# Scores of a head from one 96-row matmul over stacked high and low parts of q and k

## The reference

```python
def _L0_cond_ref(...):                     # layer L0
    q, k, v = x @ Wqkv.T + bqkv            # 16 heads of 32
    attn = softmax(einsum('bhid,bhjd->bhij', q, k) / sqrt(32))
    ...                                    # modulation by coh(x, cond), field term
    return out @ Wout.T + bout
def _L1_cond_ref(...):                     # layer L1: a key mask, no bias
    scores = where(mask, -inf, einsum(q, k) * scale)
    out = (softmax(scores) @ v) @ Wo.T
    return rmsnorm(out) * gain + shift     # the norm is on the output
def _L2_cond_ref(...):                     # layer L2: the norm is on the input
    x = x + attention(rmsnorm(x)) ; return x + swiglu(rmsnorm(x))
x = x + _L0_cond_ref(x, ...); x = x + _L1_cond_ref(x, ...); x = x + _L2_cond_ref(x, ...); ...
```

## Time and profile before

| | us |
|---|---|
| two timed runs | 3266.89 and 3268.45, median 3267.67 |
| profiled execution, span from first to last instruction | 3266.8 |
| TensorE matmul busy | 3106.6 (95%) |
| VectorE / ScalarE / GpSimd busy | 2031.8 (62%) / 1369.6 (42%) / 614.0 (19%) |
| DMA | 216.27 MB, mean 66 GB/s; 22.7% of 16 engines' span |
| one group, L0 / L1 / L2 | 46.6 / 39.9 / 38.1 |

### The profile page before, as it was taken

How to read it: one execution, slowest core, us unless ns; L and a number is a source line. 1 busy time by engine, 2 the same in 40 slices (tenths; PEclk the granted TensorE clock), 3 DMA queues, 4 the chain that set the end, 5 groups by cost and what they waited for, 6 DMA issues and landing times. The chain is left out here.

```text
span 3266.8 us, 64344 instructions
## 1 busy us (share of the span) xinstructions
PE 3106.6 (95%) x24853; PEld 2688.4 (82%) x24853; DVE 2031.8 (62%) x3739; ACT 1369.6 (42%) x2123; POOL 614.0 (19%) x340
## 2 busy tenths in 40 slices
PE   6999999998899999994999999959999999999998
PEld 5989898997788888884888989848888888888886
DVE  5666666665577777775777777755544445556544
ACT  3444444443555555553555555532222223222221
POOL 2112211220122222211111121112222221111111
PEclk8999999999999999997999999979999999999999
DMA  4221222121322222223222222241122232111111
GB/s 153 47 64 51 56 53 64 51 52 48 102 65 64 64 64 64 65 52 110 65 64 71 71 64 71 59 142 52 52 65 72 69 104 73 44 52 39 51 39 39
DMA packets 198918, 216.27 MB, mean 66 GB/s; under 512 B 17537, under 2 KB 173313, under 8 KB 198305
## 3 DMA queue, kind: packets, MB, share of 16 engines
q1 hardware_dynamic: 198816, 214.87, 22.7%
HBM read 122.53 MB, written 41.94 MB: 50 GB/s over the span
## 5 line engine op out<-in xcount | busy, mean ns | idle before, releaser
L783 ACT ACTIVATE L_pth<-L_bank_t 128x512 f16<-128x512 f32 x384 | 227.7, 593 | 380.5 <-PE L_bank_t L614 380.5
L787 ACT ACTIVATE L_shifted<-L_shifted,keep_lift 128x512 f32<-128x512 f32 x384 | 277.2, 722 | 236.6 <-DVE L_shifted L942 234.1
L1516 DVE TENSOR_TENSOR mlp_act_t<-mlp_bank_u,mlp_sg 128x512 f32<-128x512 f32 x128 | 88.5, 691 | 453.3 <-ACT mlp_sg L1418 449.6
L938 DVE TENSOR_REDUCE L_top<-L_bank_s 128x4 f32<-128x512 f32 x384 | 263.1, 685 | 129.5 <-PE L_bank_s L563 65.1
L1418 ACT ACTIVATE mlp_sg<-mlp_bank_g 128x512 f32<-128x512 f32 x128 | 76.6, 598 | 628.6 <-PE mlp_bank_u L1331 628.5
L1558 POOL TENSOR_TENSOR mlp_al<-mlp_act_t,mlp_ah 128x512 fp32r<-128x512 f32 x128 | 175.0, 1367 | 856.3 <-ACT mlp_ah L1424 856.3
L946 DVE TENSOR_TENSOR L_ptl<-L_bank_t,L_pth 128x512 f16<-128x512 f32 x384 | 262.7, 684 | 63.9 <-ACT L_pth L783 60.6
L1121 POOL TENSOR_TENSOR L_vr<-L_vf,keep_v 128x1024 f32<-128x1024 f32 x48 | 99.2, 2067 | 1045.6 <-ACT keep_v L817 1045.6
L630 PEld LDWEIGHTS L_bank_o<-keep_v,L_pth 128*128 128x128 f16 x4608 | 199.0, 96 | 97.6 <-issue 72.6
L942 DVE TENSOR_TENSOR L_shifted<-L_bank_s,L_top 128x512 f32<-128x512 f32 x384 | 265.5, 691 | 16.7
L561 PE MATMUL L_bank_a<-L_xh,L_wkh 128*128 128x256 f32 x768 | 233.7, 304 | 37.7 <-DVE L_wkl L101 24.6
(11 more groups left out here) (272 smaller groups left out, 8925.8 us busy)
## 6 DMA issues: line engine op xcount, KB each, us to landing
keep_kbh<-L_kh SPq DMA_DIRECT2D x384, 64.0 KB, 2.1
keep_kbl<-L_kl SPq DMA_DIRECT2D x384, 64.0 KB, 2.1
resid<-L_xres SPq DMA_DIRECT2D x48, 512.0 KB, 2.6
L_xf<-resid SPq DMA_DIRECT2D x32, 512.0 KB, 3.7
L_xres<-resid SPq DMA_DIRECT2D x32, 512.0 KB, 3.3
mlp_xf<-resid SPq DMA_DIRECT2D x32, 512.0 KB, 4.5
mlp_res<-resid SPq DMA_DIRECT2D x32, 512.0 KB, 4.6
L_xf<-in_x SPq DMA_DIRECT2D x16, 512.0 KB, 3.3
```

The source lines that it names most:

```text
L783: nc.scalar.activation(pth[:, u % 2], bank_t[u % 2][:].rearrange("p (h j) -> p h j", h=4), ACT.Copy).then_inc(p_high, 1)
L787: nc.scalar.activation(shifted[:, u % 2], shifted[:, u % 2], ACT.Exp, bias=k["lift"][:, 0:1], scale=SCALE).then_inc(exp_done, 1)
L938: nc.vector.reduce_max(top[:, u % 2, :], src, AX_X).then_inc(top_ready, 1)
```

## The change

The block-diagonal tile goes. For each head the parts of q and k are stacked along the partitions: `qs` holds q high, q low, q high in rows 0 to 31, 32 to 63 and 64 to 95, and `ks` holds k high, k high, k low. One matmul over these 96 rows is the sum of the three passes for one head; a unit takes four of them with 128 columns each. Both stacks are filled by DMA from `kh`, `kl`, `qh`, `ql`, 12 copies of [32 rows x 1024 elements] for k and 12 for q in a group. They hold a whole group, and there is one of each, so the copies of group i+1 wait until all eight units of group i are through, and the scores of group i+1 wait for both stacks. The projections are ordered o, k, q, v (L0: o, k, q, c, v) in place of o, k, v, q, and the first step of splitting v moves from slot 10 to slot 11. `spans`, the table of how many pieces stand in a slot, is unchanged.

```diff
-            for t in k["kbh"] + k["kbl"]:
-                nc.gpsimd.memset(f32(t[:]), 0.0)
...
-        order = [n for n in "kvcqo" if n in weights]
+        order = [n for n in ("cvo" if L0 else "kqvo") if n in weights]
...
-        fills = [(kind, half) for kind in ("okvcq" if L0 else "okvq") for half in range(2)]
+        fills = [(kind, half) for kind in ("okqcv" if L0 else "okqv") for half in range(2)]
...
-            def spread_keys(p, b):
-
-                if positive(UNITS * (p - 1) + 4 * (b + 1)):
-                    sp.wait_ge(s_full, UNITS * (p - 1) + 4 * (b + 1))
+            def stack(p, kind):
+
+                dst, high, low, done = (ks, kh, kl, ks_ready) if kind == "k" else (qs, qh, ql, qs_ready)
+                if positive(UNITS * p):
+                    sp.wait_ge(s_full, UNITS * p)
+                    sp.sem_inc(stack_begun, 1)
                 for m in range(2):
-                    sp.wait_ge(a_free[m], a_done(p, ("k", m)))
-                for dst, src in ((kbh, kh), (kbl, kl)):
+                    sp.wait_ge(a_free[m], a_done(p, (kind, m)))
+                    sp.sem_inc(stack_begun, 1)
+                for n, src in enumerate((high, high, low) if kind == "k" else (high, low, high)):
                     for h in range(4):
-                        rows = slice(HD * h, HD * (h + 1))
-                        sp.dma_start(f32(dst[b][rows, :, h, :]), f32(src[rows, :, b * P:(b + 1) * P])).then_inc(kb_ready[b], 16)
+                        sp.dma_start(f32(dst[HD * n:HD * (n + 1), h]), f32(src[HD * h:HD * (h + 1)])).then_inc(done, 16)
...
                 if u == 0:
-                    for m in range(2):
-                        pe.wait_ge(a_free[m], a_done(i, ("q", m)))
-                if c == 0:
-                    pe.wait_ge(kb_ready[b], KB_DONE * (i + 1))
-                out = bank_s[u % 2][:]
-                q_h, q_l = qh[:, c, b * P:(b + 1) * P], ql[:, c, b * P:(b + 1) * P]
-                k_h, k_l = (t[b][:, c].rearrange("p h j -> p (h j)") for t in (kbh, kbl))
-                mm = mm3(out, q_h, q_l, k_h, k_l, last=not L1)
+                    pe.wait_ge(ks_ready, STACKED * (i + 1))
+                    pe.wait_ge(qs_ready, STACKED * (i + 1))
+                part = slice(b * P, (b + 1) * P)
                 if L1:
-                    mm = nc.tensor.matmul(out.rearrange("p (h j) -> p h j", h=4), k["ident_r"][:], bcast_mid(k["mask"][:], 4), start=False, stop=True)
+                    nc.tensor.matmul(bank_s[u % 2][:].rearrange("p (h j) -> p h j", h=4), k["ident_r"][:], bcast_mid(k["mask"][:], 4),
+                                     start=True, stop=False)
+                for h in range(4):
+                    mm = nc.tensor.matmul(bank_s[u % 2][:, h * P:(h + 1) * P], qs[:, h, c, part], ks[:, h, c, part], start=not L1, stop=not L1 or h == 3)
                 mm.then_inc(s_full, 1)
...
-                    if s == 10 and has(i, 1):
+                    if s == 11 and has(i, 1):
                         first_values(i + 1)
```

More of the change, by code:

```diff
@@ L42 @@
 MASKED = -1e30
-KB_DONE = 2 * 4 * 16
+STACK = 3 * HD
+STACKED = 3 * 4 * 16
 PACKED = {"cond_t": B, "be1": CH, "bc1": CH, "bc": 2 * CH, "rms": CH, "g1b": CH, "b1b": CH, "g2b": CH, "b2b": CH,
@@ L371, in attention @@
         kh, kl = sb("kh", [P, CH, T], F32R), sb("kl", [P, CH, T], F32R)
-        kbh, kbl = k["kbh"], k["kbl"]
+        qs, ks = sb("qs", [STACK, 4, CH, T], F32R), sb("ks", [STACK, 4, CH, T], F32R)
         v1, v2, v3 = k["v1"], k["v2"], k["v3"]
@@ L530, in _ @@
                 ws.load(sp, n)
-            spread_keys(0, 0)
-            spread_keys(0, 1)
+            stack(0, "k")
+            stack(0, "q")
             sp.wait_ge(ws.low_done, len(ws.loads))
@@ L543, in body @@
                 if L1 and has(i, 1):
-                    spread_keys(i + 1, 0)
-                    spread_keys(i + 1, 1)
+                    stack(i + 1, "k")
+                    stack(i + 1, "q")
                 if positive(i):
@@ L762, in read_fill @@
                 if m == 0:
[L763 to L769, removed]
+                    if positive(STACKED * p):
+                        act.wait_ge(ks_ready if kind == "k" else qs_ready, STACKED * p)
                 if L0:
@@ L846, in _ @@
                         read_fill(0, fill)
-                if s == SLOTS - 2:
+                if s == SLOTS - 1:
                     first_values(0)
@@ L1600, in shared @@
                 return actx.enter_context(nc.sbuf_tensor("keep_" + name, shape, dt))
-            k["kbh"] = [shared(f"kbh{b}", [P, CH, 4, P], F32R) for b in range(NB)]
-            k["kbl"] = [shared(f"kbl{b}", [P, CH, 4, P], F32R) for b in range(NB)]
             for n in ("v1", "v2", "v3"):
@@ L1607, in build @@
             with ExitStack() as wctx:
-                wh, wl = weight_tiles(wctx, "L0", "kvqoc")
+                wh, wl = weight_tiles(wctx, "L0", "kqcvo")
                 k["wc2"] = wctx.enter_context(nc.sbuf_tensor("keep_wc2", [P, CH, 2 * H], F32R))
-                early = [(a["L0_" + n], flat3(wh[n]), flat3(wl[n])) for n in "kv"]
+                early = [(a["L0_" + n], flat3(wh[n]), flat3(wl[n])) for n in "kq"]
                 phase(prepare, a, early)
-                phase(attention, "L0", a["x"], scratch[0], wh, wl, {n: a["L0_" + n] for n in "cqo"})
+                phase(attention, "L0", a["x"], scratch[0], wh, wl, {n: a["L0_" + n] for n in "cvo"})
             for tag, src, dst in (("L1", scratch[0], scratch[1]), ("L2", scratch[1], scratch[2])):
@@ L1616, in build @@
                     wh, wl = weight_tiles(wctx, tag, "kvqo")
-                    phase(attention, tag, src, dst, wh, wl, {n: a[f"{tag}_{n}"] for n in "kvqo"})
+                    phase(attention, tag, src, dst, wh, wl, {n: a[f"{tag}_{n}"] for n in "kqvo"})
         phase(gated_mlp, scratch[2], scratch[1], scratch[3], out, a["gate_w"], a["hid_w"], a["out_w"])
```

2 lines of the change are left out of this document (1 added, 1 removed).

## The result

The changed kernel takes **3507.22 us** (median of 2 runs, 3506.79 to 3507.66) against 3267.67 us: ratio 1.073, 95% interval 1.070 to 1.076. The profiled execution has a span of 3505.0 us, 238.2 more than before. The forecast was 3422 us with a range of 3285 to 3510: right in direction, 85 us too low, and 3 us inside the upper end of the range.

The account below looks back on a forecast made before the run. TensorE's instruction stream, busy 95% of the span, was taken as the bound. L1 and L2 seams 14 x 4.85 + 14 x 4.6, L0 -30, -4 and +7 gave +105; clock +50 made +155 on 3266.8: 3422 us, range 3285 to 3510.

Parts of the forecast that it names:

- Mechanism of L1 and L2: At group ends, q's copies follow its low part behind the normalisation; TensorE waits: +4.85 and +4.6 us a group, 14 each.
- The copies' 9.0 us: Time for q's twelve copies until the last has landed: 9.0 us, between 6.5 and 9.9.
- plain: SyncE's issue of the new 2-dimensional copies priced at 0.35 us each, 4.2 us for twelve.
- The clock: TensorE's clock falls to half for 6.8 us behind waits in L1 and L2: +50 us, ends 0 and 95.
- 1.8 us x 28: Clock cost per group of L1 and L2: up to 3.4 us lost, less what falls into the wait.
- L0: -30 forecast: L0's 16 groups each gain 1.9 us from cheaper scores, with copies hidden: -30 us.
- It stays hidden: In L0 q's low part ends at 522.4, 14 us before the next scores, so copies cost no time.
- A unit's scores: Four 128-column matmuls take 0.46 us instead of 0.70: 0.24 us less a unit, 92 us in all.
- the gain of the scores already in it: L1's +4.85 us a group already includes the cheaper scores' saving, 1.9 us a group.
- Rest: Last groups of L1 and L2 gain (-4), layer starts lose (+7), two seams without normalisation come out even.
- the +7 for the starts of L1 and L2: At these starts only 5.6 us of v's pieces lie behind q, against 9.0 us of copies: +7 us.
- Rivals 1 to 4: The clock stays up, 3372 us, 0.20; fast copies, 3302, 0.14; hidden copies, 3236, 0.12; slow short matmuls, 3599, 0.07.

Follow-up runs that it names:

- Experiment 1: Changed kernel, VectorE making q's second low part before the normalisation's scaling, gain and shift in slot 9 of L1 and L2: 3412.71 us.
- 4: Changed kernel, SyncE issuing the eight high-part copies of q or k once ScalarE has written them, waiting only before the four low ones: 3332.14 us.
- experiment 2: Changed kernel, TensorE's two waits per group in L1 and L2 filled with 8 and 20 unused 512-column matmuls: 3441.49 us.
- experiment 7: Kernel before the change, scores alone altered to four 128-column matmuls of high parts, no low passes, added copies or waits: 3203.38 us.
- Experiment 3: Changed kernel, each of the 24 stacking copies moving 64 KB instead of 128 KB, number of copies kept: 3469.79 us.
- Experiment 6: Changed kernel, VectorE's small copy into L_fd in L0 moved from slot 0 to slot 3: 3497.7 us.
- experiment 8: Changed kernel with q's low part before the normalisation's second half, high copies issued early, and L0's L_fd copy in slot 3: 3278.78 us.

## Why the prediction was right, and where its sizes were off

1. **Mechanism of L1 and L2: right.** q's low part behind the normalisation, copies behind it, two waits a group in the places named (forecast 2.6 and 5; 2.16 and 4.95 in L1, 1.9 and 4.96 in L2). Experiment 1 takes away the first link, 4 the second; each gives about what its link costs. Without the half clock (experiment 2) L1's groups take 44.9, and 44.7 was forecast; L2's take 43.9, and 42.7 was forecast. In L2 0.5 us are the copies and 0.75 the waits for L_shifted and L_of that experiment 7 also shows (0.15, 0.29, 0.32).
2. **The copies' 9.0 us: right in size (9.5), its working only half.** An issue was priced at 0.35 us by the residual's load, because the new form is "plain". It costs 0.62, like the old key copies in the other row. Experiment 3 shows that half of the bytes take nearly as long; the forecast had named the transfer as what sets the time. That 9.0 came out was luck: the transfer's 7.1 us and the issues' 7.5 are near each other.
3. **The clock: +50 forecast, 66 measured** (experiment 2). The step that was short is "1.8 us x 28", which took half of each fall to lie in the waits. In L1 it begins with the first scores and costs 2.9 us, in L2 2.0.
4. **L0: -30 forecast, -3 measured**, a wrong step. "It stays hidden" held for the copies; what was missed is that GpSimd's L_xl now meets VectorE's small operations. Experiment 6 gives back 10 us of it. Of the rest, experiment 7 shows that L0 keeps 1.3 of 2.4 us even with neither copies nor this collision.
5. **A unit's scores: 0.46 forecast, 0.41 measured**, but "the gain of the scores already in it" counted all of 92 us. Experiment 7 has the cheap unit alone; of its 115 us 63 come through, since TensorE then waits for the chain of maximum, subtraction and exponential. A saving on the busiest engine was priced at full, with the next one close behind. The weight load that "the trace bears out" does so only by distance: loads of 128 columns in fp32r start 0.11 us apart, but each is recorded at 0.19 us.
6. **Rest: +3 forecast, 20.6 measured**: the +7 for the starts of L1 and L2 had q's copies begin with q's low part, but in L1's they stand 3.6 us behind it, after k's twelve issues in the same queue, and the two seams held to be even have one too (3.61 and 3.36 us). No run separates these.

The clock makes 16 of the 83 us that were missing, L0 27, L1 and L2 without the clock some 20, the rest 18; all but the cheaper matmul went the slow way. That the time still lies in the range, by 3 us, is luck as well: the range had room for slower copies and a dearer clock, and what filled it is L0, L2 and the rest, for which it had none. Rivals 1 to 4 fell: the clock did fall, the copies weren't fast and weren't hidden, and a short fp32r matmul isn't slow.

## What to carry to other kernels

Where data passes through a DMA between an engine that makes it and TensorE, count the issues in a row after the last part is written, at the price of that very kind of copy, and issue all that is ready sooner before it: here order alone was worth 175 us, more than the matmuls could save. A stop of TensorE can cost more than its length, since half clock may follow: 2.9 us a group behind waits of 2.16 and 5 us in L1, nothing behind L1's 1.5 us in experiment 8, and with its one wait of 1.77 us in L2 sometimes 1.3 us and sometimes nothing. And before a saving on the bounding engine is taken at full, look how far behind the next engine's chain is.

## What the runs showed of the hardware

- Issuing a copy of 32 rows within SBUF took 0.62 us on SyncE with 64 KB as with 128 KB, against 0.35 for a load of [128 rows, 512 KB] from memory; with ScalarE's queue issuing at the same time 0.75 to 0.86, and 0.78 there. Whether the number of rows or the direction makes the difference, no run shows; with 96 rows the first three took 0.51, 0.59 and 0.76.
- Copies within SBUF moved 205 GB/s at a share of 0.93 over 32 rows (an estimated 220 at full share) and 299 over 96 at a share of 1.00.
- fp32r matmuls of 128 columns with 96 rows stood 0.10 us apart, those of 256 columns 0.12.
- A VectorE COPY of 128x2 and a TENSOR_SCALAR of 128x32, SBUF to SBUF, took 1.27 and 0.86 us instead of 0.16 and 0.18 and ended within 0.04 us of GpSimd's subtraction; operations that read PSUM did not wait.
- In these seams the half clock stood in the rows for 3.4 or 6.8 us. Behind the scores 3.4 us cost 1.3 to 1.5 us (38.5 and 39.8 in L2 of experiment 8, 44.5 and 46.0 in L1 of experiment 3), 6.8 us 2.9 (L1 of experiment 2); ahead of a wait it shortened the wait (4.59 to 2.99 us).
